# Layer-norm passes of an early-fusion kernel: from GpSimd to the vector engine, two units sooner

## The chip, the cores and the metric

One core of a Trainium2 chip runs the whole program. The metric is the device time of one launch in microseconds (us). Three runs of the kernel before took 2034.75, 2037.20 and 2037.57 us; the median is 2037.2 us.

## What is computed

64 sequences of 48 tokens (16 image patches, 32 text tokens) are embedded into 192 features. Then a bidirectional Mamba block and a mixture of 8 experts follow, each behind a layer norm and with a residual:

```python
h = concatenate([tok(patches), txt(ids, position, age, segment)], axis=1)
h = h + attn(layernorm(h))     # attn ends in its own layer norm, with gain ln_g and bias ln_b
h = h + ffn(layernorm(h))      # the 2 best of 8 experts for each token
```

Inside `attn`, with m the two Mamba directions summed and projected, the result is `layernorm(m + x) * ln_g + ln_b`. The change concerns the normalising passes of this second layer norm (called h2 in the kernel) and of the third, `layernorm(h)` in front of the experts (called x3).

## The kernel before, in words

The 3072 tokens go through the embedding and the Mamba part in 8 chunks (0 to 7) of 8 sequences, 384 tokens, held as three tiles of 128 partitions by 192 features. The expert part follows when all chunks are done.

**Units.** The Mamba scan of a chunk is cut into 24 units: 2 directions, 3 tiles of 128 channels, 4 groups of 4 states. In each unit ScalarE writes the decays into PSUM (`act_decay`, L603), GpSimd multiplies the input of the scan into a ring of four buffers (`pool_input`, L619, the product at L629), the vector engine (DVE) runs two scans and two products (`dve_scan`, L640 and L642, in the order scan, product, scan, product), and TensorE sums the states (`pe_sum`, L652). GpSimd works two units ahead: its product for unit w+2 is issued in unit w and waits for the first scan of unit w (L628) and for the sum of unit w-2 (L627).

**Order.** All five engines walk one written-out plan (`plan`, L925). For each unit w it gives the product for w+2 ("ahead"), the gates, the scan of w, the decays of w+1, the DMAs that spread B and C, the sum of w-1, and then the steps put into slot w. While chunk c is scanned, the slots hold the back end of chunk c-1 (`BACK`, L917), the front end of chunk c+1 (`FRONT`, L909), and the projections of the directions (`DIR0`, `DIR1`). An engine takes the steps that it has an entry for, in this order. Plans 0 and 1 are written out, plans 2 to 6 are a loop, plan 7 is written out without a front end; a last, unscanned stretch (`epilogue`, L1007) does the back end of chunk 7.

**The back end before**, by slot: 3 and 4, DVE adds the residual and takes mean and variance (`dve_out`, `dve_stat`); 5, ScalarE takes the reciprocal root (`act_rs`, L704); 6, `norm_h2` (L710): three tensor_scalar passes of 128x192 with two per-partition scalars (L715), one multiplication by ln_g (L718) and one addition of the kept h (L721), both 128x576; SP stores the result. 8, DVE takes the statistics of the third norm (`dve_stat3`, L723) and ScalarE the root (`act_rs3`, L734); 9, `norm_x3` (L740): three more passes (L746), and SP stores x3. 15 to 23, transposes and the router. `norm_h2` and `norm_x3` run on GpSimd for chunks 0 to 6, which are the back ends in plans 1 to 7, and on DVE for chunk 7 in the epilogue.

**Beside them.** Slot 6 also has GpSimd's "keep" (L288, one 128x576 addition), behind h2. Slot 5 has ScalarE's sines with two table loads (`act_sin`, L368). Slot 7 has the embedding on DVE (`dve_embed`, L382; its L391 reads img_t and proj_bias from SBUF), slot 8 its `x1` (L430, three passes like L715), slot 9 of direction 1 the DVE's four step-time passes (`dve_steps`, L568, at L570, L573, L575, L577). The gate in front of unit 9 (`dve_gate`, L658) waits for the sum of unit 7.

Of the kernel before, what the change touches and what calls it, by code (L numbers as in the profile page):

```python
# [63 lines left out]
def wait(eng, sem, value):  # L64

    if isinstance(value, int) and value <= 0:
        return
    eng.wait_ge(sem, value)


def build_mamba(nc, a, dram, ident, logits, sem):

    with ExitStack() as ctx:
        def sb(name, shape, dt=F32):

            return ctx.enter_context(nc.sbuf_tensor(name, shape, dt))
# [70 lines left out]
        h2 = sb("h2", [128, NT, D])  # L147
        x3 = sb("x3", [128, NT, D])
# [61 lines left out]
        dv = Steps(sem("dir_dve"), "conv0a conv1a conv2a conv0b conv1b conv2b m w1 r dt")  # L210
        ds = Steps(sem("dir_act"), "silu x0 exp0 x1 exp1 ln")
        qv = Steps(sem("back_dve"), "stat aggr stat3 aggr3")
        qp = Steps(sem("back_pool"), "norm gain h2 x3")
        qa = Steps(sem("back_act"), "ln rs ln3 rs3")


# [36 lines left out]
        def alone(eng):  # L253


            eng.sem_inc(passes[eng.engine.name], 1)
# [18 lines left out]
        def pool_rows(gp, c):  # L275

            gp.wait_ge(ids_in, 32 * c + 32)
            wait(gp, fv.sem, fv.after("txt3", c - 1))
            alone(gp)
            for t in range(2):  # L280
                gp.indirect_dma_start(tok_rows[:, t, :], None, a["tok_emb"], bass.IndirectOffsetOnAxis(ap=ids[:, t:t + 1], axis=0)).then_inc(rows_in, 16)
                gp.indirect_dma_start(seg_rows[:, t, :], None, a["seg_emb"], bass.IndirectOffsetOnAxis(ap=ids[:, 2 + t:3 + t], axis=0)).then_inc(rows_in, 16)
# [55 lines left out]
        def whole_turns(eng, c):  # L338

            eng.wait_ge(fp.sem, fp.after("theta", c))  # L340
            wait(eng, qfull, QJ * (c - 2))
            alone(eng)
            for s in range(2):
                o = eng.tensor_scalar(turns[:, s], theta[:, s], 1.0 / TWO_PI, 0.25 if s == 0 else 0.0, ALU.mult, ALU.add)
            o.then_inc(fp.sem, 1)
            eng.wait_ge(fp.sem, fp.after("turn", c))
            alone(eng)
            eng.tensor_scalar(turns[:], turns[:], MAGIC, -MAGIC, ALU.add, ALU.add).then_inc(fp.sem, 1)
# [361 lines left out]
        def norm_h2(eng, c):  # L710

            eng.wait_ge(qa.sem, qa.after("rs", c))
            alone(eng)
            for t in range(NT):
                o = eng.tensor_scalar(h2[:, t, :], h2[:, t, :], qmv[:, t, 0:1], qrs[:, 1, t:t + 1], ALU.subtract, ALU.mult)  # L715
            o.then_inc(qp.sem, 1)
            eng.wait_ge(qp.sem, qp.after("norm", c))
            eng.tensor_tensor(h2[:], h2[:], ln_g[:].unsqueeze(1).to_broadcast([128, NT, D]), ALU.mult).then_inc(qp.sem, 1)  # L718
            eng.wait_ge(qp.sem, qp.after("gain", c))
            eng.wait_ge(hb_ok, c + 1)  # L720
            eng.tensor_tensor(h2[:], h2[:], hb[:], ALU.add).then_inc(qp.sem, 1)  # L721
# [18 lines left out]
        def norm_x3(eng, c):  # L740
            eng.wait_ge(qa.sem, qa.after("rs3", c))
            wait(eng, x3_out, 16 * c)
            wait(eng, qfull, QJ * (c - 1) + 4)
            alone(eng)
            for t in range(NT):
                o = eng.tensor_scalar(x3[:, t, :], h2[:, t, :], qmv[:, t, 0:1], qrs[:, 1, t:t + 1], ALU.subtract, ALU.mult)  # L746
            o.then_inc(qp.sem, 1)
# [70 lines left out]
        def pool_setup(gp):  # L818
            gp.memset(ones[:], 1.0)
            gp.memset(ident[:], 0.0).then_inc(set_pool, 1)  # L820
            gp.memset(spare, 0.0).then_inc(set_pool, 1)
            gp.wait_ge(set_pool, 2)
            gp.affine_select(out=ident[:], in_=ident[:], compare_op=ALU.not_equal, fill=1.0, base=0, pattern=[[-1, 128]], channel_multiplier=1).then_inc(set_pool, 1)
# [71 lines left out]
        def set_up(eng):  # L895
# [18 lines left out]
        DIR1 = {-2: ["x01"], -1: ["x01_out", "x2"], 0: ["x2_out", "conv01"],  # L914
                1: ["z01", "conv2", "silu", "z01_out"], 2: ["bc", "bc_out"], 3: ["bc_store"], 5: ["dt0"],
                7: ["dt0_out", "dt12"], 8: ["dt12_out", "softplus", "z2"], 9: ["z2_out", "steps"]}
        BACK = {2: ["out01"], 3: ["out01_add", "out2"], 4: ["out2_add"], 5: ["rs"], 6: ["h2"],  # L917
                8: ["stat3", "rs3"], 9: ["x3"], 15: ["x3T0"], 17: ["x3T0_out", "x3T1"], 19: ["x3T1_out"],
                20: ["router"], 23: ["logits"]}
        KEEP = 6  # L920
        KEPT = 12
# [3 lines left out]
        def plan(c, first, last):  # L925
# [4 lines left out]
            def put(stage, at, chunk, k):  # L930
                for w, names in stage.items():
                    if 0 <= at + w < U2:
                        slots[at + w] += [(s, chunk, k) for s in names]
# [19 lines left out]
            if not first:  # L953
                put(BACK, 0, c - 1, 0)
            slots[KEEP].append(("keep", c, 0))
# [25 lines left out]
        def in_order(stage, c, k):  # L981
            return [(s, c, k) for w in sorted(stage) for s in stage[w]]
# [24 lines left out]
        def epilogue():  # L1007
            c = NCH - 1
            yield "sum", c, U2 - 1
            yield "gate", c, (1, NC - 1)  # L1010
            yield from in_order(BACK, c, 0)

        def at_start(c):

            return isinstance(c, int) and c == 0

        def at_end(c):

            return isinstance(c, int) and c == NCH - 1
# [6 lines left out]
        def program(eng, steps):  # L1026

            run(eng, steps, early())
            if "folded" in steps:
                steps["folded"](eng)  # L1030
            set_up(eng)
            run(eng, steps, prologue())
            run(eng, steps, plan(0, True, False))
            run(eng, steps, plan(1, False, False))
            with eng.Fori(2, NCH - 1) as c:
                run(eng, steps, plan(c, False, False))
            run(eng, steps, plan(NCH - 1, False, True))
            run(eng, steps, epilogue())

        @block.sync  # L1040
        def _(sp):
            sp_setup(sp)

            sp.wait_ge(set_pool, 3)
            sp.dma_start(dram["x3"][NTOK:NTOK + 128, :], spare).then_inc(filled, 16)

            sp.dma_start(dram["out"][NTOK:NTOK + 128, :], spare[:, 0:D]).then_inc(filled, 16)
            program(sp, {
                "load": lambda e, c, k: sp_load(e, c),
                "h2": lambda e, c, k: sp_store(e, c, "h2"),  # L1050
                "x3": lambda e, c, k: sp_store(e, c, "x3"),
                "bc_store": lambda e, c, d: sp_bc(e, c, d),
                "spread": lambda e, c, k: sp_spread(e, c, *k),
            })
            sp.wait_ge(h2_out, 16 * NCH)
            sp.wait_ge(x3_out, 16 * NCH)
            sp.wait_ge(filled, 32)

        @block.gpsimd
        def _(gp):  # L1060
            pool_setup(gp)
            pool_rows(gp, 0)
            gp.wait_ge(w_in, LOADED)
            program(gp, {
                "rows": lambda e, c, k: pool_rows(e, c),
                "phase": lambda e, c, k: (pool_phase(e, c), None if at_start(c) else whole_turns(e, c)),
                "keep": lambda e, c, k: pool_keep(e, c),
                "kept": lambda e, c, k: pool_kept(e, c),
                "ahead": pool_input,
                "h2": lambda e, c, k: None if at_end(c) else norm_h2(e, c),  # L1070
                "x3": lambda e, c, k: None if at_end(c) else norm_x3(e, c),
            })

        @block.scalar
# [23 lines left out]
        @block.vector  # L1098
        def _(v):
            dve_setup(v)  # L1100
            program(v, {
                "phase": lambda e, c, k: (dve_patch_stats(e, c), whole_turns(e, c) if at_start(c) else None),
                "reduce": lambda e, c, k: dve_reduce(e, c),
                "embed": lambda e, c, k: dve_embed(e, c),
                "x1": lambda e, c, k: dve_x1(e, c),
                "conv01": lambda e, c, d: dve_conv(e, c, d, (0, 1)),
                "conv2": lambda e, c, d: dve_conv(e, c, d, (2,)),
                "steps": dve_steps,
                "scan": dve_scan, "gate": lambda e, c, k: dve_gate(e, c, *k),
                "out01_add": lambda e, c, k: dve_out(e, c, (0, 1)),  # L1110
                "out2_add": lambda e, c, k: (dve_out(e, c, (2,)), dve_stat(e, c)),
                "h2": lambda e, c, k: norm_h2(e, c) if at_end(c) else None,
                "stat3": lambda e, c, k: dve_stat3(e, c),
                "x3": lambda e, c, k: norm_x3(e, c) if at_end(c) else None,
                "logits": lambda e, c, k: dve_router(e, c),
            })

# [545 lines left out]
```

## Time and profile before

| | |
|---|---|
| runs (3) | 2034.75, 2037.20, 2037.57 us; median 2037.2 us |
| profiled execution | 2037.6 us, span 2035.9 us |
| busy, share of the span | PE 75%, DVE 74%, POOL 52%, ACT 42% |
| DVE in the 40 slices | 9 tenths in nearly all of the first 29, 1 to 5 tenths after them |
| granted TensorE clock, mean | 0.857 of full speed |

POOL is GpSimd, PE is TensorE, ACT is ScalarE. A timeline row reads: start in us, length in us (of the whole run where several are merged), engine, line, operation, tile written <- tiles read, count, and in brackets the engine's idle time just before and who ended it. Starts of following instructions on one engine lie closer than their lengths, since instructions overlap at their ends.

### The profile page before, as it was taken

How to read it: one execution, taken by the hardware profiler on the slowest of the kernel's cores; microseconds unless marked ns; L12 is line 12 of the kernel's file. 1: busy time of each engine (PE TensorE's matmuls, PEld its weight loads, DVE VectorE, ACT ScalarE, POOL GpSimd, SP SyncE). 2: the span in 40 equal slices, each digit the busy share in tenths (PEclk: the TensorE clock that was granted, in tenths of full speed). 3: DMA queues.
4: the chain of work that ended last, by engine and by line, in shares of the span. 5: the costliest groups of instructions: out<-in, count | busy, mean ns of one | idle time of the engine just before them, and what ended most of it. 6: DMA issues, size and time to landing. Idle time of an engine off the chain costs nothing. (4 is left out here: it accounts for less than half of the span.)

```text
span 2035.9 us, 19521 instructions
## 1 busy us (share of the span) xinstructions
PE 1523.3 (75%) x4714; PEld 866.1 (43%) x4715; DVE 1514.1 (74%) x1780; ACT 861.1 (42%) x1848; POOL 1056.5 (52%) x539
## 2 busy tenths in 40 slices
PE   6566776776677677767767775876643899999997
PEld 4233343343344334434433443443332566666665
DVE  3699999999999999999999999999954122222221
ACT  2555545554554555455455454554510222222221
POOL 2465676675667657655675675548600233333332
PEclk8777897888788778878878887888875999999999
DMA  3412303031231303122130402213025411111111
GB/s 80 148 48 79 119 29 136 21 129 52 85 114 35 136 16 133 38 99 97 53 120 18 147 37 100 85 42 136 0 73 133 114 26 24 25 24 24 26 24 22
DMA packets 49182, 144.71 MB, mean 71 GB/s; under 512 B 13118, under 2 KB 26028, under 8 KB 48332
## 3 DMA queue, kind: packets, MB, share of 16 engines
q1 hardware_dynamic: 36956, 129.61, 18.7%
q0 software_dynamic: 12144, 14.30, 4.2%
q14 instruction: 66, 0.54, 0.1%
q8 instruction: 16, 0.26, 0.1%
HBM read 132.67 MB, written 11.21 MB: 71 GB/s over the span
## 5 line engine op out<-in xcount | busy, mean ns | idle before, releaser
L629 POOL TENSOR_TENSOR ring<-dtu,brep 128x1536 f32<-128x1536 f32 x192 | 661.0, 3447 | 446.0 <-DVE states L640 316.3
L652 PE MATMUL py<-ring,ident 128*128 128x384 f32 x1536 | 637.2, 568 | 133.7 <-DVE yg L669 110.5
L640 DVE TENSOR_TENSOR_SCAN states<-states,ring 128x768 f32<-128x768 f32 x384 | 673.7, 1755 | 30.2 <-ACT states L616 14.7
L652 PEld LDWEIGHTS py<-ring,ident 128*128 128x128 f32 x1536 | 332.7, 223 | 420.6 <-issue 186.2
L616 ACT ACTIVATE states<-dt_,aneg 128x376 f32<-128x376 f32 x768 | 406.1, 560 | 0.0
L642 DVE TENSOR_TENSOR ring<-states,crep 128x768 f32<-128x768 f32 x384 | 367.6, 957 | 13.2
L613 ACT ACTIVATE states<-zero_cols 128x16 f32<-128x16 f32 x384 | 71.2, 186 | 642.7 <-DVE ring L642 637.6
L1288 PE MATMUL gu<-w,xsT 96*128 x660 | 298.3, 602 | 7.2 <-issue 6.6
L462 PE MATMUL pf<-xT,wxz 97*128 97x384 f32 (+1 forms) x384 | 183.7, 624 | 139.0 <-ACT xT L449 55.3
L1329 DVE COPY yidx<-place 128x1 int32 (+1 forms) x56 | 8.4, 153 | 250.8 <-DMA out_tokens<-ys,yidx 250.8
L1288 PEld LDWEIGHTS gu<-w,xsT 96*128 96x128 f32 x660 | 122.6, 193 | 145.6 <-issue 145.6
L1269 POOL DMA_INDIRECT xs<-x_scratch,yidx x56 | 55.4, 990 | 244.3 <-PE xps L1275 127.0
L462 PEld LDWEIGHTS pf<-xT,wxz 97*128 97x128 f32 (+1 forms) x384 | 87.5, 239 | 218.6 <-ACT xT L449 60.0
L1345 POOL DMA_INDIRECT out_tokens<-ys,yidx x55 | 87.3, 1588 | 127.1 <-DVE ys L1324 64.8
L1294 ACT ACTIVATE act_g<-gu 128x768 f32<-128x768 f32 x55 | 44.6, 811 | 253.8 <-PE gu L1288 253.8
L495 DVE SCALAR_TENSOR_TENSOR ea<-xc,cw,ea 128x384 f32<-128x384 f32 x144 | 119.7, 859 | 11.0 <-ACT ea L477 8.7
L1299 DVE TENSOR_TENSOR hid<-act_g,gu 128x768 f32<-128x768 f32 x55 | 52.5, 954 | 87.1 <-ACT act_g L1294 87.1
L1317 PE MATMUL yps<-wd,hidT 128*128 x660 | 116.4, 326 | 1.0 <-ACT hidT L1311 1.0
L1317 PEld LDWEIGHTS yps<-wd,hidT 128*128 128x128 f32 x660 | 105.9, 190 | 1.7 <-issue 1.7
L519 PE MATMUL pf<-u,xpw 128*44 128x384 f32 x96 | 51.7, 696 | 62.0 <-ACT u L510 40.2
L624 POOL TENSOR_TENSOR dtu<-dt_,u 128x384 f32<-128x384 f32 x48 | 47.9, 998 | 92.2 <-DVE dt_ L577 92.2
L543 PE MATMUL pf<-proj,dtw 12*128 12x384 f32 x96 | 58.0, 711 | 45.1 <-ACT dtu L553 44.6
(221 smaller groups left out, 1412.3 us busy)
## 6 DMA issues: line engine op xcount, KB each, us to landing
brep<-b_c_rows SPq DMA_DIRECT2D x64, 768.0 KB, 4.1
crep<-b_c_rows SPq DMA_DIRECT2D x64, 768.0 KB, 4.6
w<-in_w SPq DMA_DIRECT2D x8, 1152.0 KB, 14.2
wd<-in_wd SPq DMA_DIRECT2D x8, 576.0 KB, 16.3
ptok<-in_p_tok SPq DMA_DIRECT2D x8, 384.0 KB, 3.8
pT<-in_p_T SPq DMA_DIRECT2D x8, 384.0 KB, 4.8
out_tokens<-h SPq DMA_DIRECT2D x8, 288.0 KB, 2.1
x_scratch<-x SPq DMA_DIRECT2D x8, 288.0 KB, 2.9
```

Of the source, the lines that this page charges most:

```text
L462: mm = pe.matmul(p[:, 0:T], wxz[0:rows, d, k, 128 * o:128 * o + 128], xT[0:rows, k].rearrange("p b l -> p (b l)"), start=(k == 0), stop=(k ...
L495: op = v.scalar_tensor_tensor(acc, x, cw[:, o, k:k + 1], acc, ALU.mult, ALU.add)
L543: pe.matmul(p[:, 0:T], dtw[2 * NS:2 * NS + R, 128 * o:128 * o + 128], proj[2 * NS:2 * NS + R, :], start=True, stop=True).then_inc(jsem(f"d ...
L613: act.activation(start, zero_cols[:].unsqueeze(2), ACT.Copy)
L616: op = act.activation(x0[:, k, :, lo:lo + L - 1], src, ACT.Exp, scale=aneg[:, o, n:n + 1])
L629: gp.tensor_tensor(ring[:, w % NRING], dtu[:, d, o, :].unsqueeze(1).to_broadcast([128, GN, T]), brep[:, ng], ALU.mult).then_inc(dbu_ok, 1)
L640: v.tensor_tensor_scan(h_in, h_in, x_in, 0.0, ALU.mult, ALU.add).then_inc(scan_ok, 1)
L642: v.tensor_tensor(x, h, half_of(crep[:, ng], i), ALU.mult).then_inc(hc_ok, 1)
L652: mm = pe.matmul(py[:, 0:T], ident[:], ring[:, w % NRING, i, :], start=(ng == 0 and i == 0), stop=False)
L1288: mm = pe.matmul(gu[:, 512 * n:512 * n + 512], xsT[:, b, k, :], w13[:, bass.ds(e, 1), k, 512 * n:512 * n + 512].rearrange("p a n -> p (a n ...
L1317: mm = pe.matmul(yps[:, 0:D], hidT[:, b, 128 * k:128 * k + 128], wd[:, bass.ds(e, 1), k, :].rearrange("p a n -> p (a n)"), start=(k == 0), ...
L1345: gp.indirect_dma_start(dram["out"], bass.IndirectOffsetOnAxis(ap=yidx[:, r:r + 1], axis=0), ys[:, b, :], None, compute_op=ALU.add).then_i ...
```

## The change

The vector engine does `norm_h2` and `norm_x3` for every chunk; GpSimd has no entry for them any more. `dve_stat3` follows `norm_h2` in slot 6 (it was in slot 8), `act_rs3` is in slot 7 (8), and `norm_x3` with its store in slot 8 (9). The passes themselves, their tiles and the epilogue's order are as they were. The semaphore is renamed.

```diff
-        qp = Steps(sem("back_pool"), "norm gain h2 x3")
+        qp = Steps(sem("back_norms"), "norm gain h2 x3")
...
-        BACK = {2: ["out01"], 3: ["out01_add", "out2"], 4: ["out2_add"], 5: ["rs"], 6: ["h2"],
-                8: ["stat3", "rs3"], 9: ["x3"], 15: ["x3T0"], 17: ["x3T0_out", "x3T1"], 19: ["x3T1_out"],
+        BACK = {2: ["out01"], 3: ["out01_add", "out2"], 4: ["out2_add"], 5: ["rs"], 6: ["h2", "stat3"],
+                7: ["rs3"], 8: ["x3"], 15: ["x3T0"], 17: ["x3T0_out", "x3T1"], 19: ["x3T1_out"],
                 20: ["router"], 23: ["logits"]}
...
@@ block.gpsimd
-                "h2": lambda e, c, k: None if at_end(c) else norm_h2(e, c),
-                "x3": lambda e, c, k: None if at_end(c) else norm_x3(e, c),
...
@@ block.vector
-                "h2": lambda e, c, k: norm_h2(e, c) if at_end(c) else None,
+                "h2": lambda e, c, k: norm_h2(e, c),
                 "stat3": lambda e, c, k: dve_stat3(e, c),
-                "x3": lambda e, c, k: norm_x3(e, c) if at_end(c) else None,
+                "x3": lambda e, c, k: norm_x3(e, c),
```

## Rows read from the trace of the kernel before

**Rows 1.** Busy time by engine (page, part 1).

```profile
PE 1523.3 (75%) x4714; PEld 866.1 (43%) x4715; DVE 1514.1 (74%) x1780; ACT 861.1 (42%) x1848; POOL 1056.5 (52%) x539
```

**Rows 2.** Busy time in stretches: plan 3. Columns: length, PE, PEld, DVE, ACT, POOL, clock.

```profile
616.00:797.00 181.00, 129.36 (x352) 71.20 (x353) 172.21 (x176) 93.13 (x208) 116.12 (x54) 0.82 0.22 80
```

**Rows 3.** Timeline of DVE, units 6 to 10 of plan 2.

```profile
483.18 0.96 DVE L642 TENSOR_TENSOR ring<-states,crep 128x768 f32<-128x768 f32 x1
485.95 1.77 DVE L640 TENSOR_TENSOR_SCAN states<-states,ring 128x768 f32<-128x768 f32 x1 [1.81 <-ACT states L616]
...
491.99 2.96 DVE L391 SCALAR_TENSOR_TENSOR h_new<-img_t,prs,proj_bias 128x192 f32<-128x192 f32 x1 [0.30 <-DVE img_t L386]
...
504.03 0.87 DVE L726 BATCH_NORM_STATS2 qst<-h 128x6 f32<-128x192 f32 x3
...
505.47 0.96 DVE L430 TENSOR_SCALAR x_new<-h_new,hmv,hrs 128x192 f32<-128x192 f32 x3
...
512.21 1.35 DVE L570 SCALAR_TENSOR_TENSOR dt_<-dtu,dt_ 128x1152 f32<-128x1152 f32 x1
...
517.35 1.75 DVE L640 TENSOR_TENSOR_SCAN states<-states,ring 128x768 f32<-128x768 f32 x1
```

**Rows 4.** Timeline of POOL (GpSimd), the same stretch.

```profile
484.02 3.00 POOL L715 TENSOR_SCALAR h<-h,qmv,qrs 128x192 f32<-128x192 f32 x3
...
489.95 1.40 POOL L288 TENSOR_TENSOR hb_next<-h_new,ln_b 128x576 f32<-128x576 f32 x1
491.30 3.44 POOL L629 TENSOR_TENSOR ring<-dtu,brep 128x1536 f32<-128x1536 f32 x1
...
512.15 6.16 POOL L746 TENSOR_SCALAR x<-h,qmv,qrs 128x192 f32<-128x192 f32 x3
```

**Rows 5.** Timeline of ACT and of PE, the same stretch.

```profile
480.28 0.21 ACT L708 ACTIVATE qrs<-qrs 128x3 f32<-128x3 f32 x1
...
499.67 0.81 PE L655 MATMUL py<-u,skip_diag 128*128 128x384 f32 x2
```

**Rows 6.** Timeline of DVE, plan 0 and plan 1 (L391), second half of plan 2 (steps).

```profile
139.78 0.42 DVE L391 SCALAR_TENSOR_TENSOR h_new<-img_t,prs,proj_bias 128x192 f32<-128x192 f32 x1
...
313.21 3.31 DVE L391 SCALAR_TENSOR_TENSOR h_new<-img_t,prs,proj_bias 128x192 f32<-128x192 f32 x1
...
593.18 1.35 DVE L570 SCALAR_TENSOR_TENSOR dt_<-dtu,dt_ 128x1152 f32<-128x1152 f32 x1
...
598.03 1.76 DVE L640 TENSOR_TENSOR_SCAN states<-states,ring 128x768 f32<-128x768 f32 x1
```

**Rows 7.** Timeline of DVE, plan 7: first scan of unit 7, gate before unit 9.

```profile
1384.89 1.75 DVE L640 TENSOR_TENSOR_SCAN states<-states,ring 128x768 f32<-128x768 f32 x1
...
1398.93 0.62 DVE L669 TENSOR_TENSOR yg<-py,zs 128x128 f32<-128x128 f32 x2 [2.07 <-PE py L655]
```

**Rows 8.** Timeline of DVE, epilogue: the same passes, GpSimd idle.

```profile
1501.83 0.96 DVE L715 TENSOR_SCALAR h<-h,qmv,qrs 128x192 f32<-128x192 f32 x3 [0.72 <-ACT qrs L708]
1502.83 0.76 DVE L718 TENSOR_TENSOR h<-h,ln_g 128x576 f32<-128x576 f32 x1
1503.62 0.76 DVE L721 TENSOR_TENSOR h<-h,hb 128x576 f32<-128x576 f32 x1
```

**Rows 9.** Timeline of POOL and of DVE in the setup.

```profile
21.00 2.04 POOL L335 TENSOR_TENSOR theta<-theta,b_tau 128x384 f32<-128x384 f32 x2
...
21.15 1.05 DVE L843 TENSOR_SCALAR gw<-brep,crep 128x192 f32<-128x192 f32 x1
...
23.05 0.31 DVE L843 TENSOR_SCALAR gw<-brep,crep 128x192 f32<-128x192 f32 x1
23.27 0.28 DVE L844 TENSOR_SCALAR crep<-ones,crep 128x128 f32<-128x128 f32 x1
```

**Rows 10.** Groups of DVE instructions by line and shape: busy us, mean ns.

```profile
L1324 DVE TENSOR_SCALAR ys<-yps,yweight 128x192 f32<-128x192 f32 x55 | 23.0, 418 | 24.5 <-PE yps L1317 24.5
...
L430 DVE TENSOR_SCALAR x_new<-h_new,hmv,hrs 128x192 f32<-128x192 f32 x24 | 7.7, 376 | 1.2 <-ACT hrs L421 0.7
```

## The prediction

> **What bounds the kernel now.** I read the busy times by engine first: no engine stands out over the whole span (PE 75%, DVE 74%) [rows 1]. The busy times by stretch separate the stages: in one plan of the loop, 181.0 us long, DVE is busy for 172.2 us, GpSimd for 116.1, ACT for 93.1 [rows 2]. So in the Mamba part DVE sets the pace, and a microsecond added to its queue counts unless it fills a hole that is there now. The expert part isn't touched. Then I read the timelines of DVE and GpSimd side by side, from unit 6 to unit 10 of plan 2, where the moved steps lie [rows 3, 4]; plans 3 to 6 repeat this stretch to within some hundredths. Three costs of the present arrangement show there. DVE is free at 484.06, when the last product of unit 6 ends (its follower starts 0.88 after 483.18 wherever there is no wait), but unit 7 starts at 485.95: a hole of 1.81 us, ended by ACT's decays. L391 takes 2.96 us. And the step-time passes take 5.14 us from 512.21 to 517.35.
>
> **What is removed.** *The hole.* ACT's sines delay the decays of unit 7, and they still will; but DVE has the h2 passes to do there, so the hole is filled: 1.81 us of the new work is free. *L391.* Alone it takes 0.42 us [rows 6]. In plan 2 it starts at 491.99 and ends at 494.95, just after GpSimd's ring product, which runs from 491.30 to 494.74 [rows 4]. That product is late because GpSimd does h2 and keep first. Without h2 it starts behind the first scan of unit 7 and takes 3.44 us, which is what DVE needs for the rest of unit 7; so L391 is free again, as in plan 0: 2.54 us back in plans 2 to 6, 2.89 in plan 1 [rows 6]. Plan 7 has no embedding and gets nothing. *x3 on GpSimd.* Undisturbed, the steps take 4.85 us (593.18 to 598.03) [rows 6], beside GpSimd's L746 they take 5.14: 0.29 back.
>
> **What is added, in slot 6.** In the epilogue the three L715 passes take 1.00 us until L718 starts, L718 takes 0.79 to the next start, and L721 is the same kind and size: 2.58 us [rows 8]. dve_stat3 moves from slot 8 to slot 6 with its 1.44 us (504.03 to 505.47) [rows 3]. The reciprocal root that L715 waits for is there at 480.49 [rows 5], long before 484.06.
>
> GpSimd isn't idle then: keep (L288, 1.40 us) [rows 4] now follows the ring product directly and takes the place of L715, at 484.02. Does it hold DVE up? No row shows a two-scalar pass beside GpSimd. The bounds: nothing, if DVE isn't held or holds GpSimd instead; at most keep's whole 1.40. The nearest row is the setup's L843, a one-scalar pass of the same 128x192: 0.31 us alone, 1.05 us when GpSimd's two-input L335 had started 0.15 before; it ended 0.18 after that instruction's half of the 2.04 us [rows 9]. Is L715 of this kind? L844 and L843 differ by 64 elements and 0.03 us, half a nanosecond for an element [rows 9]; L1324, which reads PSUM with one scalar, takes 418 ns, and L430, with two scalars from SBUF, only 376 [rows 10]. So L430, and L715 with it, run at the fast rate that L843 has, and I take the hold: keep ends at 485.42, the first pass at 485.60, the others 0.59 later, L718 at 486.23, L721 at 487.02, stat3 at 487.81, and unit 7 starts at 489.25, 3.30 us later than now. Against an unheld start this costs 1.17 us a plan.
>
> The Trainium skill, VectorE: DVE Perf Modes, section "Mode 2×_2P — use both read ports for one tensor", says that a single-source fp32 pass in SBUF with an even width reads through both ports, and gives no exception for per-partition scalars. By that rule L715 is of L843's kind and the sum is the one below; without it, the first rival's. L843 agrees with it for one scalar; no row here shows it for two.
>
> **What follows, in plans 2 to 6.** 3.30 late at unit 7; minus 2.54 at L391 leaves 0.76 at unit 8. In slot 8 stat3's 1.44 are gone and x3's three passes come in, 0.96 as for L430 [rows 3]: 0.28 left. The steps give 0.29 back. The plan ends 0.01 us early: nothing. Plan 1 gains 0.35 more at L391.
>
> **Plan 7** has neither hole nor embedding. Unit 7 starts at 1384.89 now [rows 7]; the h2 block, its hold and stat3 put it 5.19 later (489.25 less 484.06). DVE then waits 2.07 us for the sum of unit 7 in front of unit 9. That sum hangs on unit 7, since TensorE has a projection before it that waits for ACT, and ACT for the products of unit 7; so it moves along by 5.19 and the wait stays. x3's 0.96 and the missing stat3 lie inside it. The steps give 0.29 back: 4.9 us are lost.
>
> **At no cost.** In the loop the same gate is reached at 506.4 now (505.47 and the 0.96 of L430) [rows 3], and would be at 506.7; its sum ends at 500.48 [rows 5] and moves 3.30 to 503.8. The cover is 2.9 us; beyond that each plan would pay. act_rs3 goes ahead of the embedding's root on ACT, 0.5 us where ACT waits for DVE anyhow. SP's two stores (one DMA each) wait for earlier events than now, and the spreads queued behind them wait for ring products and scans that come later still. On GpSimd everything behind h2 and x3 comes sooner; it waits for DVE in each unit. The epilogue is unchanged.
>
> **The sum.** Five times nothing, minus 0.35, plus 4.9: plus 4.5 us. The profiled execution took 2037.6 us (span 2035.9, and 1.7 around it), 0.4 above the median; so 2042.1 in its terms, 2041.7 against the median, and I write 2041.5. That is at the edge of 0.2% (4.1 us), about what a measurement of this kernel can tell from no change.
>
> **Rivals.** *First, L715 isn't held*, and only L718 waits for the last 0.36 us of keep. For it: no row has two scalars. Against it: the rates above. It saves 0.81 us in each of 7 plans, 5.7 us: 2035.8, not slower.
>
> *Second, DVE wins against keep.* L746 on GpSimd started at 512.15, before DVE's L570 at 512.21; L570 took its usual 1.35 us, and the three L746 took 6.16 where three L715 take 3.00 [rows 3, 4]. So there GpSimd was held. Against it: L746 has one input, and L335 and the ring product, with two like keep, held DVE. It saves 1.17 in 7 plans, 8.2 us: 2033.3, where faster begins.
>
> The Trainium skill, SBUF — State Buffer, section "SBUF: two separate sides", says that whichever of the two engines starts first keeps the shared ports for its whole instruction. By that rule keep wins with its 0.04 us of lead and the forecast holds; the L746 rows don't agree with it, so this rival keeps a chance.
>
> *Third, slower: gaps at the waits in the loop.* L391 has five waits in front of it and shows 0.30 us of idle time in the loop [rows 3] and none in plans 0 and 1, where no register holds the chunk [rows 6]. If L715, L718, L721 and L746 each pay the 0.30, five looped plans lose 6.0 us more: 2047.5. Against it: those four have one to three waits, and L718 and L721 follow within 0.04 us in the epilogue [rows 8]. It decides from a mean gap of 0.1 us.
>
> **Chances.** Forecast 0.55, half of it on either side of the 0.2% bound; first rival 0.20, all within; second 0.12, of which 0.11 beyond it on the fast side; third 0.13. So faster 0.11, same 0.48 (0.27, 0.20 and 0.01), slower 0.41 (0.28 and 0.13). The range leaves out the outer part of the second and the far end of the third: 2033.5 to 2046.5.
>
> **What would show it.** Right: in plans 2 to 6 no wait for ACT in front of unit 7, its start 5.2 us behind the end of unit 6, the first L715 at 1.5 us and its two followers at 0.37; L391 at 0.42; steps at 4.85; the gate of unit 9 without a wait; plan 7 some 5 us longer. Wrong: L715 at 0.37 beside keep, a gate that waits in the loop, idle time in front of L718 and L721, or an L391 that is still held.

## The result and the profile after

The changed kernel takes 2043.55 us (median of 8 runs, 2042.42 to 2045.06), the kernel before 2037.62 us beside it (8 runs): a ratio of 1.0030, 95% interval 1.0019 to 1.0041. That is 5.9 us slower, where 4.5 were forecast in the sum and 2041.5 us was written. The profiled execution took 2043.2 us, its span 2041.5 us, against 2037.6 and 2035.9 before: 5.6 us.

The busy times by engine, kernel after (to be read against [rows 1]):

```profile
PE 1524.4 (75%) x4714; PEld 865.8 (42%) x4715; DVE 1523.2 (75%) x1836; ACT 861.2 (42%) x1848; POOL 973.8 (48%) x483
```

GpSimd lost 56 instructions and 82.7 us of work, DVE got the 56 and only 9.1 us more, since it does the passes faster and its L391 is no longer held. The busy shares say nothing about the end; the stretch of units 6 to 10 does. Timeline of DVE, kernel after, the stretch of [rows 3]:

```profile
482.72 0.96 DVE L642 TENSOR_TENSOR ring<-states,crep 128x768 f32<-128x768 f32 x1
483.60 2.02 DVE L715 TENSOR_SCALAR h<-h,qmv,qrs 128x192 f32<-128x192 f32 x3
485.65 0.76 DVE L718 TENSOR_TENSOR h<-h,ln_g 128x576 f32<-128x576 f32 x1
486.45 0.76 DVE L721 TENSOR_TENSOR h<-h,hb 128x576 f32<-128x576 f32 x1
487.24 0.88 DVE L726 BATCH_NORM_STATS2 qst<-h 128x6 f32<-128x192 f32 x3
...
488.60 1.77 DVE L640 TENSOR_TENSOR_SCAN states<-states,ring 128x768 f32<-128x768 f32 x1
...
494.64 0.42 DVE L391 SCALAR_TENSOR_TENSOR h_new<-img_t,prs,proj_bias 128x192 f32<-128x192 f32 x1 [0.30 <-DVE img_t L386]
...
498.80 1.76 DVE L640 TENSOR_TENSOR_SCAN states<-states,ring 128x768 f32<-128x768 f32 x1
...
504.13 0.95 DVE L746 TENSOR_SCALAR x<-h,qmv,qrs 128x192 f32<-128x192 f32 x3
505.00 0.95 DVE L430 TENSOR_SCALAR x_new<-h_new,hmv,hrs 128x192 f32<-128x192 f32 x3
505.87 0.62 DVE L669 TENSOR_TENSOR yg<-py,zs 128x128 f32<-128x128 f32 x2
506.40 1.75 DVE L640 TENSOR_TENSOR_SCAN states<-states,ring 128x768 f32<-128x768 f32 x1
...
516.57 1.75 DVE L640 TENSOR_TENSOR_SCAN states<-states,ring 128x768 f32<-128x768 f32 x1
```

The hole of 1.81 us in front of unit 7 is gone: the first L715 starts when the last product of unit 6 ends, and unit 7 starts 5.00 us after that, without a wait. L391 takes 0.42 us, the gate of unit 9 (L669) has no wait, and from the end of unit 6 (483.60) to unit 10 (516.57) DVE is busy nearly throughout. The L715 group takes 2.02 us where it takes 0.96 alone [rows 8]. Its three passes one by one (shortest, median and longest in ns, then the first and the last start):

```profile
L715 DVE TENSOR_SCALAR h<-h,qmv,qrs x3: 368/369/1445, 483.6 to 485.3; 128x192 f32<-128x192 f32 x3
```

The whole delay is in the first pass. Timeline of GpSimd, kernel after, the stretch of [rows 4]:

```profile
480.10 3.46 POOL L629 TENSOR_TENSOR ring<-dtu,brep 128x1536 f32<-128x1536 f32 x1 [0.94 <-DVE states L640]
483.52 1.40 POOL L288 TENSOR_TENSOR hb_next<-h_new,ln_b 128x576 f32<-128x576 f32 x1
490.45 3.43 POOL L629 TENSOR_TENSOR ring<-dtu,brep 128x1536 f32<-128x1536 f32 x1 [5.53 <-DVE states L640]
```

Keep starts 0.08 us ahead of L715, takes its usual 1.40 us and ends at 484.92; the first L715 pass ends 0.12 us after it, at 485.04, and the two others follow at their usual length. So keep holds one pass. The ring product, which lay on L391 before, now runs from 490.45 to 493.88, ahead of it.

In plan 7 the same block finds neither hole nor embedding. Timelines of DVE and then of TensorE, kernel after, plan 7 (to be read against [rows 7]); the third fence is TensorE in the kernel before:

```profile
1382.07 2.09 DVE L715 TENSOR_SCALAR h<-h,qmv,qrs 128x192 f32<-128x192 f32 x3
...
1387.41 1.73 DVE L640 TENSOR_TENSOR_SCAN states<-states,ring 128x768 f32<-128x768 f32 x1
...
1401.98 0.62 DVE L669 TENSOR_TENSOR yg<-py,zs 128x128 f32<-128x128 f32 x2 [2.99 <-PE py L655]
```

```profile
1394.57 1.64 PE L543 MATMUL pf<-proj,dtw 12*128 12x384 f32 x2 [9.97 <-ACT dtu L553]
1396.14 5.06 PE L652 MATMUL py<-ring,ident 128*128 128x384 f32 x8
```

```profile
1392.06 1.64 PE L543 MATMUL pf<-proj,dtw 12*128 12x384 f32 x2 [4.64 <-ACT dtu L553]
1393.63 4.52 PE L652 MATMUL py<-ring,ident 128*128 128x384 f32 x8
```

In both kernels the projection starts 7.2 us behind the first scan of unit 7 (1394.57 less 1387.41; 1392.06 less 1384.89) [rows 7]: the sum that the gate waits for moved along with unit 7. Its eight matmuls took 0.54 us longer besides. The wait grew by 0.92 us, from 2.07 to 2.99: those 0.54, and 0.38 since DVE gets there sooner, with x3's 0.95 in the place of stat3's 1.33.

**Where the 5.6 us of the profiles went.** Differences of first-scan starts, unit 6 to unit 10:

| us | plan 1 | plans 2 to 6, each | plan 7 | sum of 7 plans | experts | span |
|---|---|---|---|---|---|---|
| before | 38.40 | 38.60 to 38.62 | 30.46 | 261.9 | 520.9 | 2035.9 |
| after | 37.77 | 38.29 to 38.31 | 35.95 | 265.2 | 523.8 | 2041.5 |
| forecast difference | -0.36 | -0.01 | +4.9 | +4.5 | 0 | |
| measured difference | -0.63 | -0.3 | +5.5 | +3.3 | +2.9 | +5.6 |

"Experts" is the stretch from the router's first integer cast to the last instruction. What is left, -0.6 us, is in the other stretches. So in this pair of profiles the moved steps cost 3.3 us, by two opposite terms as forecast, and 2.9 us lie in a stage whose steps the change leaves as they were. The first figure repeats: over two profiles of the kernel after and three of the kernel before it is 3.3 to 3.7. The others don't: the expert part differs by 1.0 to 3.0 us between them, and what is left took 1249.7 to 1253.1 us in the three profiles of the kernel before alone.

### The profile page after: what moved, and what is told of

Its sections match the earlier page's. It is cut to its first block and busy times, and to the rows that moved or that the text cites. A ratio compares the mean times of both kernels' runs of the same rounds, so it can differ in the third digit from the quotient of the medians.

```text
span 2041.5 us, 19516 instructions
## 1 busy us (share of the span) xinstructions
PE 1524.4 (75%) x4714; PEld 865.8 (42%) x4715; DVE 1523.2 (75%) x1836; ACT 861.2 (42%) x1848; POOL 973.8 (48%) x483
## 5 line engine op out<-in xcount | busy, mean ns | idle before, releaser
L462 PE MATMUL pf<-xT,wxz 97*128 97x384 f32 (+1 forms) x384 | 174.5, 598 | 121.3 <-ACT xT L449 53.4
L462 PEld LDWEIGHTS pf<-xT,wxz 97*128 97x128 f32 (+1 forms) x384 | 83.1, 227 | 198.0 <-ACT xT L449 58.2
L519 PE MATMUL pf<-u,xpw 128*44 128x384 f32 x96 | 56.3, 749 | 68.0 <-ACT u L510 44.5
```

Of the source, the lines that this page charges most:

```text
L462: mm = pe.matmul(p[:, 0:T], wxz[0:rows, d, k, 128 * o:128 * o + 128], xT[0:rows, k].rearrange("p b l -> p (b l)"), start=(k == 0), stop=(k ...
```

## The experiments

In each run the ratio is to the kernel before, timed beside it. "Stretch" is the length from unit 6 to unit 10 as in the table. Differences to the kernel after are between medians of separate sittings, in which the kernel before read 2035.88 to 2037.62 us. A kernel's median less the sum of its seven stretches lies between 1775.3 us (e5_before_keep_early) and 1778.8 (e7_keep_one_input), with 1775.7 for the kernel before and 1778.3 for the one after; so the stretches account for the medians to within 3.5 us.

**Keep out of the way (e1_keep_early).** The kernel after, with GpSimd's keep in slot 4 in place of 6.

```diff
+            slots[KEEP - 2].append(("keep_pool", c, 0))
...
-                "keep": lambda e, c, k: pool_keep(e, c),
+                "keep_pool": lambda e, c, k: pool_keep(e, c),
```

> The changed kernel with GpSimd's keep (L288) moved from slot 6 to slot 4, so that it no longer runs beside the h2 passes on DVE. Theory (keep holds the first L715 pass): the three L715 passes take 0.96 us in place of 2.02, unit 7 starts 1.06 us earlier in each of 7 plans, 7.4 us in all: about 2036 us, level with the kernel before. Rival (the passes are slow in the loop for another reason, waits or registers): they stay at 2.02 us and the time at 2043.6.

Measured: 2035.15 us (11 runs), ratio 0.9991 (0.9982 to 1.0000), 8.4 us under the kernel after. Timelines of DVE and GpSimd, e1_keep_early, plan 2:

```profile
482.27 0.95 DVE L715 TENSOR_SCALAR h<-h,qmv,qrs 128x192 f32<-128x192 f32 x3
```

```profile
469.21 1.41 POOL L288 TENSOR_TENSOR hb_next<-h_new,ln_b 128x576 f32<-128x576 f32 x1
```

With keep gone, L715 falls from 2.02 to 0.95 us, and the stretch from 38.30 to 37.23 in plans 2 to 6: all of the 1.07. In plan 7 only 0.57 comes back (35.95 to 35.38), as the gate waits 0.57 longer there. The seven stretches give back 7.1 us, near the 7.4 expected. The hold was real, and keep was its cause.

**The last plan as before (e2_last_gpsimd).** The kernel after, but the back end of plan 7 stays on GpSimd in the old slots.

```diff
+        BACK_LAST = {2: ["out01"], 3: ["out01_add", "out2"], 4: ["out2_add"], 5: ["rs"], 6: ["h2"],
+                     8: ["stat3", "rs3"], 9: ["x3"], 15: ["x3T0"], 17: ["x3T0_out", "x3T1"], 19: ["x3T1_out"],
+                     20: ["router"], 23: ["logits"]}
...
-                put(BACK, 0, c - 1, 0)
+                put(BACK_LAST if last else BACK, 0, c - 1, 0)
...
+                "h2": lambda e, c, k: norm_h2(e, c) if in_last(c) else None,
+                "x3": lambda e, c, k: norm_x3(e, c) if in_last(c) else None,
...
@@ block.vector
-                "h2": lambda e, c, k: norm_h2(e, c),
+                "h2": lambda e, c, k: None if in_last(c) else norm_h2(e, c),
...
-                "x3": lambda e, c, k: norm_x3(e, c),
+                "x3": lambda e, c, k: None if in_last(c) else norm_x3(e, c),
```

> The changed kernel, but in plan 7 alone the old arrangement (h2 in slot 6 and x3 in slot 9 on GpSimd, stat3 and rs3 in slot 8). Theory (plan 7 has no hole to fill and no embedding, and pays the whole of the moved work): plan 7 from unit 7 on is as in the kernel before, 5.5 us come back, about 2038 us. Rival (the loss beyond the sum lies in the expert part or is spread over the plans): less than 3 us come back, 2041 or more.

Measured: 2037.18 us (11 runs), ratio 0.9999 (0.9990 to 1.0008), 6.4 us under the kernel after. The stretch of plan 7 is 30.29 us again, plans 1 to 6 are those of the kernel after (37.75, 38.30). So plan 7 alone carries the loss of the moved steps, and six plans with a hole and an embedding gain 2.2 us together (0.65 and five times 0.3). That gain doesn't show in the median: in this profile the expert part took 522.5 us, 1.6 more than in the first one of the kernel before.

**Keep, but with one input (e7_keep_one_input).** As the kernel after; keep multiplies by a constant and leaves out the addition of ln_b, so the values behind it differ.

```diff
-            gp.tensor_tensor(hb_next[:], h_new[:], ln_b[:].unsqueeze(1).to_broadcast([128, NT, D]), ALU.add).then_inc(hb_next_ok, 1)
+            alone(gp)
+            gp.tensor_scalar(hb_next[:], h_new[:], 1.0, None, ALU.mult).then_inc(hb_next_ok, 1)
```

> The changed kernel with keep in its place as a GpSimd pass of one input (hb_next = h_new * 1.0; the addition of ln_b is left out). If only two-input GpSimd instructions hold DVE, the three L715 passes take about 1.0 us, keep is stretched instead, and the time is about 2036 us. If any GpSimd instruction that starts first holds DVE, the first L715 pass waits for keep's whole length, 0.7 to 1.0 us, and the time is 2041 to 2043 us.

Measured: 2042.07 us (9 runs), ratio 1.0021 (1.0011 to 1.0031). Timelines of DVE and GpSimd, e7_keep_one_input, plan 2 (its lines are one further down):

```profile
482.86 1.69 DVE L716 TENSOR_SCALAR h<-h,qmv,qrs 128x192 f32<-128x192 f32 x3
```

```profile
482.78 1.65 POOL L289 TENSOR_SCALAR hb_next<-h_new 128x576 f32<-128x576 f32 x1
```

The three passes one by one:

```profile
L716 DVE TENSOR_SCALAR h<-h,qmv,qrs x3: 366/699/780, 482.9 to 483.8; 128x192 f32<-128x192 f32 x3
```

A GpSimd pass with one input holds L715 as well, by 0.73 us (1.69 less 0.96) where the two-input keep holds it by 1.06. But the first pass didn't wait for keep's whole length, which the second case expected: it took 0.70 us, and two of the three were done by 483.85, while keep ran on to 484.44. Keep took 1.65 us itself; how long it takes alone no run here shows.

**Keep twice (e8_keep_twice).** As the kernel after; one more keep, into a tile that nothing reads, just ahead of keep.

```diff
+        hb_twice = sb("hb_twice", [128, NT, D])
...
+            alone(gp)
+            gp.tensor_tensor(hb_twice[:], h_new[:], ln_b[:].unsqueeze(1).to_broadcast([128, NT, D]), ALU.add)
```

> The changed kernel with keep done twice in slot 6, the first time into a tile that nobody reads. Theory (DVE's first free-standing pass waits for as much GpSimd work as stands there): the L715 group grows from 2.02 us by 1.36, once in each of 7 plans, 9.5 us: about 2053 us. If DVE gets a pass in between the two keeps, the hold is the same in sum, but spread over two passes. Rival (keep's hold is a fixed delay of some 1 us, whatever its length): the time stays within 2 us of 2043.6.

Measured: 2048.96 us (5 runs), ratio 1.0049 (1.0035 to 1.0063), 5.4 us above the kernel after, between the 9.5 that the theory expected (about 2053 us) and the 2 at most of its rival; the traces decide between them. Timelines of DVE and GpSimd, e8_keep_twice, plan 2 (L718 is the kernel after's L715):

```profile
486.21 3.11 DVE L718 TENSOR_SCALAR h<-h,qmv,qrs 128x192 f32<-128x192 f32 x3
```

```profile
486.12 1.43 POOL L290 TENSOR_TENSOR hb_twice<-h_new,ln_b 128x576 f32<-128x576 f32 x1
487.48 1.44 POOL L291 TENSOR_TENSOR hb_next<-h_new,ln_b 128x576 f32<-128x576 f32 x1
```

The three passes one by one:

```profile
L718 DVE TENSOR_SCALAR h<-h,qmv,qrs x3: 368/1450/1453, 486.2 to 489.0; 128x192 f32<-128x192 f32 x3
```

Now two passes take 1.45 us: DVE gets one pass in between the two keeps, and each keep holds one. No keep, one, two: 0.95, 2.02, 3.11 us, so each keep of 1.4 us costs DVE three quarters of its length. The expectation had the second keep cost 1.36, nearly its whole length. The stretch grows by the same 1.09 in plans 2 to 6 (38.30 to 39.39) and by 1.18 in plan 7 (35.95 to 37.13), 7.7 us in all: what DVE is held is on the path. The profiled spans differ by 7.6 us (2049.1 and 2041.5), the medians by 5.4; the five runs lay between 2044.15 and 2051.29 us.

**The kernel before with keep early (e5_before_keep_early).** The edit of e1_keep_early on the kernel before: if keep only delayed GpSimd's ring product there, L391 must come partly free.

> The kernel before with GpSimd's keep alone moved from slot 6 to slot 4. Theory (L391 is held by the late ring product, which is late by h2 and by keep): the ring product for unit 9 starts 1.35 us earlier and L391 takes 1.6 us in place of 2.96; 1.35 us back in plans 1 to 6, about 8 us: 2029.5 us. Rival (L391 waits for something else, or keep costs DVE as much in slot 4): 2037.6, within 2 us.

Measured: 2029.33 us (5 runs), ratio 0.9962 (0.9949 to 0.9976). Timelines of DVE and GpSimd, e5_before_keep_early, plan 2:

```profile
491.36 1.60 DVE L391 SCALAR_TENSOR_TENSOR h_new<-img_t,prs,proj_bias 128x192 f32<-128x192 f32 x1 [0.30 <-DVE img_t L386]
```

```profile
489.31 3.44 POOL L629 TENSOR_TENSOR ring<-dtu,brep 128x1536 f32<-128x1536 f32 x1
```

The ring product ends at 492.75 and L391, 0.21 us after it, at 492.96; its 2.96 us [rows 3] were that product's tail. One moved addition is worth 7.8 us to the kernel before (its stretch falls from 38.60 to 37.21), and with it in place the norms' move is still a loss: e1_keep_early, which is this plus the move, takes 5.8 us longer. 4.1 of that are in the stretches: plan 7 is 4.4 longer (35.38 and 31.00), the six others 0.3 shorter together.

**Both repairs (e3_last_and_keep), and the best version (e6_h2_dve_x3_gpsimd).** The first is the two edits of e1 and e2 together. The second leaves x3 on GpSimd in slot 9 for chunks 0 to 6 besides:

```diff
-                7: ["rs3"], 8: ["x3"], 15: ["x3T0"], 17: ["x3T0_out", "x3T1"], 19: ["x3T1_out"],
+                7: ["rs3"], 9: ["x3"], 15: ["x3T0"], 17: ["x3T0_out", "x3T1"], 19: ["x3T1_out"],
...
-                "x3": lambda e, c, k: norm_x3(e, c) if in_last(c) else None,
+                "x3": lambda e, c, k: None if at_end(c) else norm_x3(e, c),
...
@@ block.vector
-                "x3": lambda e, c, k: None if in_last(c) else norm_x3(e, c),
+                "x3": lambda e, c, k: norm_x3(e, c) if at_end(c) else None,
```

> Both edits of the two experiments before together: plan 7 in the old arrangement and keep in slot 4. Theory (two separate costs that add): units 6 to 10 take 37.2 us in plans 2 to 6 (38.6 before), plan 7 about 31.0; about 2029 us. Rival (the early keep gives the same few microseconds once, whatever else is undone): about 2035 us.

> As the run before, but x3 of the looped plans and plan 1 stays on GpSimd in slot 9. Theory (only the h2 passes have a hole to fill; x3 costs DVE 0.87 us and its absence gives back 0.29): units 6 to 10 take 36.6 us in plans 2 to 6, 0.58 less than with x3 on DVE, 3.5 us in six plans: about 2025.5 us. Rival (x3 on GpSimd holds DVE's step-time passes more than that, or delays the ring product): no faster than the run before.

Measured: 2030.8 us (5 runs), ratio 0.9961 (0.9947 to 0.9975), and 2025.47 us (5 runs), ratio 0.9945 (0.9932 to 0.9959). Both are under both kernels; the second is the fastest of all, 18 us under the kernel after. Timelines of DVE and GpSimd, e6_h2_dve_x3_gpsimd, plan 2:

```profile
484.06 0.95 DVE L715 TENSOR_SCALAR h<-h,qmv,qrs 128x192 f32<-128x192 f32 x3
...
494.03 0.42 DVE L391 SCALAR_TENSOR_TENSOR h_new<-img_t,prs,proj_bias 128x192 f32<-128x192 f32 x1 [0.30 <-DVE img_t L386]
```

```profile
510.21 6.14 POOL L746 TENSOR_SCALAR x<-h,qmv,qrs 128x192 f32<-128x192 f32 x3
```

h2 on DVE fills the hole unheld and L391 is free; x3 on GpSimd is held again (6.14 us), which costs DVE 0.30 us in its steps where the passes on DVE cost 0.87. The stretch falls from 37.23 to 36.67 by that, the difference of the two. The stretches of the seven plans sum to 249.9 us, 12.0 under the kernel before; the medians differ by 10.4. Against e5_before_keep_early, which has the early keep and no norm moved, it is 3.9 us faster (4.1 in the stretches), and e3_last_and_keep, with x3 moved too, 1.5 us slower (0.9 faster in the stretches). So in plans 1 to 6 moving h2 (with stat3) pays, and moving x3 takes most of that away.

**Is the expert part's length the norms' doing? (before_again, after_again, before_third, e9_late_experts).** The first three have no edit. The last is the kernel before with nine more statistics passes on DVE in the epilogue, into a tile that nothing reads, so that the experts start later.

```diff
+        qst_more = sb("qst_more", [128, 3 * NT, 6])
...
+            if at_end(c):
+                for t in range(3 * NT):
+                    v.bn_stats(qst_more[:, t, :], h2[:, t % NT, :])
```

> The kernel before, profiled once more. In its first profile the stretch from the first router pass to the end took 520.9 us, in the changed kernel's 523.8. If the expert part differs from run to run, whatever the kernel, this run shows a length between 521 and 525, not 520.9 again; if the change made it longer, it is within 0.5 of 520.9. Units 6 to 10 of the looped plans take 38.6 us either way.

> The changed kernel, profiled once more. Units 6 to 10: 37.8 us in plan 1, 38.3 in plans 2 to 6, 36.0 in plan 7, as in its first profile. The expert part: between 521 and 525 us if it differs from run to run, within 0.5 of 523.8 if the change made it longer.

> The kernel before, profiled a third time. The expert part took 520.9 and 520.8 us so far. If that is a property of this program, it is within 0.5 of 520.9 again; if it varies from run to run it lies between 521.5 and 525.

> The kernel before with nine more statistics passes on DVE in the epilogue alone (2.4 us, into a tile that nobody reads): the expert part starts about 2.4 us later behind an unchanged Mamba part. If the expert part's length depends on where its stalls fall against the clock steps, and on nothing that the change moved, it can come out anywhere from 520.8 to 524.7 us and the time at 2039 to 2043; if 520.9 belongs to the old arrangement of the norms, it stays within 0.5 of that and the time is 2.4 us above the kernel before.

Measured: 2033.95, 2042.34 and 2037.68 us, one execution each; e9_late_experts 2040.33 us (11 runs), ratio 1.0018 (1.0009 to 1.0027): 3.2 us, of which the passes explain 2.3, by which its epilogue is longer. The expert part took 520.8 us in before_again, 523.7 in after_again and 522.7 in before_third, and the stretches of units 6 to 10 stayed as they were within 0.3 us in sum. The first two came out as they should if the change had made the part longer; the third did not, since with nothing changed it took 1.8 us more. With the norms as before, e9_late_experts has 523.8 us of experts, the kernel after's length. Over all thirteen profiles the eight with plan 7's norms as before lie between 520.8 and 523.8 us, the five with them on DVE between 523.7 and 524.7. The difference arises at the third tile of tokens; timelines of TensorE there, kernel before, then kernel after, then e9_late_experts, then before_third:

```profile
1595.00 1.54 PE L1305 MATMUL hps<-ident,hid 128*128 128x128 f32 x6 [6.56 <-DVE hid L1299]
1596.34 6.35 PE L1288 MATMUL gu<-w,xsT 96*128 x12
```

```profile
1599.44 1.54 PE L1303 MATMUL hps<-ident,hid 128*128 128x128 f32 x6 [7.61 <-DVE hid L1297]
1600.78 7.64 PE L1286 MATMUL gu<-w,xsT 96*128 x12
```

```profile
1594.44 1.54 PE L1309 MATMUL hps<-ident,hid 128*128 128x128 f32 x6 [7.55 <-DVE hid L1303]
1595.78 7.74 PE L1292 MATMUL gu<-w,xsT 96*128 x12
```

```profile
1593.59 1.54 PE L1305 MATMUL hps<-ident,hid 128*128 128x128 f32 x6 [6.57 <-DVE hid L1299]
1594.93 7.90 PE L1288 MATMUL gu<-w,xsT 96*128 x12
```

In the kernel after TensorE waits 1.05 us longer for the tile than in the kernel before, and the twelve matmuls behind the wait take 1.29 us longer: 2.3 of the 2.9 us. The slower matmuls can come without the longer wait: before_third waits as long as the kernel before, and its twelve matmuls take 1.55 us longer. The wait goes back to a DMA. DVE makes `hid` only after its copy of the next tile's row numbers, and that copy waits until an earlier tile's scatter to `out_tokens` has landed. Timelines of DVE, kernel before, then kernel after:

```profile
1593.65 0.15 DVE L1329 COPY yidx<-place 128x1 int32<-128x1 int32 x1 [12.91 <-DMA out_tokens<-ys,yidx]
```

```profile
1598.09 0.15 DVE L1327 COPY yidx<-place 128x1 int32<-128x1 int32 x1 [14.06 <-DMA out_tokens<-ys,yidx]
```

The granted clock in the stretch around the wait (third last column), kernel before and then kernel after:

```profile
1582.00:1600.00 18.00, 11.44 (x37) 6.64 (x37) 1.59 (x5) 1.89 (x3) 3.86 (x3) 0.81 0.93 233
```

```profile
1585.00:1604.00 19.00, 11.39 (x35) 6.56 (x34) 1.59 (x5) 1.97 (x4) 4.14 (x3) 0.77 0.80 196
```

Both are means between the two levels, 1.2 and 2.4 GHz (0.5 and 1.0): in the kernel after more of the stretch is at the lower one. What decides when the scatter lands, and how long the clock stays low behind the wait, is open. before_third and e9_late_experts show that the part gets longer with the norms as before; that their place in plan 7 makes it likelier is not excluded by the thirteen profiles.

## Why the prediction was right or wrong, point by point

- **The hole**: right. It was filled, and the sines no longer cost DVE anything.
- **Keep holds L715**: right, and it was the largest choice of the sum. 2.05 us from the first L715 to L718 against 2.17 forecast, the first pass at 1.45 us and its two followers at 0.37, as the forecast had it. e1_keep_early takes the hold away by taking keep away, e8_keep_twice doubles it. The two-scalar pass behaves as L843 does [rows 9], as the Trainium skill, VectorE: DVE Perf Modes, section "Mode 2×_2P — use both read ports for one tensor", has it for fp32 passes with a single source in SBUF. In the prediction that was an argument from rates, and e1_keep_early and e8_keep_twice show the hold itself (which ports it is about, no run shows). The first rival, no hold, falls with them.
- **Who wins**: GpSimd, by 0.08 us of lead; the second rival falls. The Trainium skill, SBUF — State Buffer, section "SBUF: two separate sides", has whichever starts first keep the shared ports for the whole instruction. With two inputs the kernel after agrees: the first pass ends 0.12 us after keep (485.04 and 484.92), and the others follow it. With one input it does not: keep started first in e7_keep_one_input too, but two of the passes were done 0.59 us ahead of its end (483.85 and 484.44).
- **L391**: right, 0.42 us, and the reason too: in e5_before_keep_early the ring product starts 1.35 us sooner behind unit 6, and L391 shortens by 1.36.
- **Unit 7 in the loop**: 3.11 us late, not 3.30. L715's group was 0.12 shorter, since keep had 0.08 us of lead, not 0.04, and the first pass ended 0.12 after it, not 0.18 (the forecast had that from half of a merged row [rows 9]). stat3 was 0.08 shorter (1.36 to the scan, not 1.44). Unit 8 follows 10.20 us after unit 7, not 12.74: the 2.54 of L391 to the hundredth. x3 for stat3 brings 0.59, not 0.48, since x3's passes take 0.87 to the next start. The steps give 0.30 back, forecast 0.29. 3.11 less 2.54, 0.59 and 0.30 is -0.32: each plan gains 0.3 us, not 0.01. This is a mis-sized term: plans 1 to 6 gain 2.15 us in sum, 1.7 more than forecast.
- **Gaps at the waits in the loop**, the third rival: it falls. L718 and L721 start 0.03 and 0.04 us behind the end of the group ahead of them, L746 and L715 at once.
- **The gate in the loop**: no wait. The sum's last matmul ended at 503.60, 2.3 us ahead of L669 in plan 2; a cover of 2.9 us was forecast.
- **Plan 7**: right in its mechanism. The block and stat3 put unit 7 5.34 us later against 5.19 (the second wait of stat3 took 0.5 us there), the gate 0.53 more than forecast as the sum's matmuls ran 0.54 us longer, and the steps gave 0.38 back: 5.5 us against 4.9. e2_last_gpsimd shows that this plan alone makes the move a loss.
- **"The expert part isn't touched"**: the step that failed. None of its steps is touched, and so I put it at nothing; but its length isn't a constant. It took 520.8 to 524.7 us over the thirteen profiles, 520.8 to 522.7 in those of the kernel before, and 2.9 us more in the first profile of the kernel after than in the first one before. I had only one profile of it and no measure of its spread. The time came out slower by over 0.2% (the interval begins at 0.19%), which had 0.41, and not within it, the likeliest by 0.48: with the moved steps alone (+3.3 us) it would have stayed within.

The forecast of 2041.5 us was 2 us short. In the profiles two misses of opposite sign met: 1.2 us too much for the moved steps, 2.9 too little for the experts, with 0.6 the other way elsewhere. The rest is that the kernel before read 2037.62 us beside the changed one, 0.4 above the median that the forecast was added to, that the medians lie 0.3 further apart than the profiles, and 0.2 of rounding. That the moved steps lose was right for the reason given in plan 7; that the time came out near is in part chance.

## What to carry to other kernels

When work moves onto the engine that sets the pace, look in every plan separately for the hole it is to fill: the last plan, which has none, paid more than the six others gained. Look, too, at what the relieved engine does in that moment: a GpSimd addition that nobody waited for came onto DVE's path, 1.07 us a plan, because it slid under the passes that had moved; two slots earlier it gave 8 us in either kernel. Move steps one by one: here h2 gained on DVE and x3 did not. In this case half of a difference of 0.3% between two profiles lay in a stage whose steps were the same, and that stage differed by 1.8 us between profiles of one kernel; so measure such a stage in repeated profiles before a sum is called right or wrong to the microsecond.

## What the runs showed of the hardware that was not expected

- Three DVE passes of 128x192 with two per-partition scalars take 0.95 us alone, 1.69 beside a GpSimd pass with one input, 2.02 beside one with two, 3.11 beside two of these. A two-input GpSimd addition of 1.40 us held exactly one pass, until 0.12 us after its own end. Three GpSimd passes of the same shape with one input (L746) take 6.14 us against 3.00 when DVE's step-time passes (three with two inputs, one with one) run beside them, and cost DVE 0.30. So in one pairing GpSimd holds DVE, and in the other DVE holds GpSimd more than it is held.
- Eight fp32 matmuls of the sum took 4.52 us in the kernel before and 5.06 after TensorE had been idle for 9.97 us, not 4.64, ahead of the projection. But they took 5.05 in e5_before_keep_early too, with 4.64 of idle time. The twelve behind the experts' wait took 6.35 us after 6.56 idle, 7.90 after 6.57, 7.64 after 7.61 and 7.74 after 7.55. So at the same wait the work behind it took 6.35 or 7.90 us; the length of the wait alone doesn't tell.
- A stage of 521 us, with the same instructions, took 520.8 to 522.7 us in three profiles of one kernel and up to 524.7 in the others (0.8%). Nearly all of the spread arises in its first three tiles of 55.
